# A fused attention and FP4 feed-forward layer on one core: fifty products into an unread bank, placed in TensorE's waits of the last two slots

## The chip, the core and the metric

The kernel runs on one core of a Trainium2 chip. The metric is the device time of one execution in microseconds (us). The kernel before takes 616.92 us, the median of three runs (615.69, 616.92 and 621.15 us). The profiled execution took 619.32 us. Engines: TensorE (PE, with its weight loads as PEld), VectorE (DVE), ScalarE (ACT), GpSimd (POOL) and the DMA queue that SyncE (SP) feeds.

## The reference, cut to what matters

Eight sequences of 512 rows by 256 columns go through two blocks, each with a residual connection:

```python
x = x + xattn(layernorm(x), ctx)      # causal self attention, cross attention, relu FFN, three layernorms
x = x + ffn(layernorm(x))             # SwiGLU, every operand quantised in blocks of 16 to FP4 and back
# ffn: gate = fp4(x) @ fp4(w_gate).T ; up = fp4(x) @ fp4(w_up).T
#      h = silu(gate) * up ; out = fp4(h) @ fp4(w_down).T
```

Widths: the model has 256 columns, the relu layer 1024, the FP4 layer 704. Every operand of the large products is split into a high and a low part (hi, lo), and three products (hi·hi, hi·lo, lo·hi) stand for one.

## The kernel before, in words

The rows are cut into 16 pairs of 256 rows (two blocks, t = 0 and t = 1, of 128 rows each). A pair goes through four stages, each one slot later than the one before: self-attention scores (lag 0), values and cross attention (lag A = 1), the relu feed-forward (lag F = 2), and the FP4 feed-forward (lag Q = 3), whose last part, the down projection, reaches into the slot after (lag Q + 1). So every slot works on up to five pairs at once. The work of each engine is written out by hand in the order in which it is to run (one `slot` function for each engine, called by `slots`, L281), and semaphores tie the engines together. An engine never passes a waiting instruction of its own: what stands behind it waits too.

The last slots are emptier. The pairs are numbered 0 to 15, PAIRS is 16, and the last slots are:

- slot 18 (PAIRS + 2): the second part of pair 14's down stage, and gate and up products of pair 15, nothing else;
- slot 19 (PAIRS + 3): the down stage of pair 15 alone.

TensorE's order in slot 18: `down(t=0)` of pair 14 (18 products of 256 columns, L1075 to L1077), `turn_hq(t=1)` (6 transposes, L886), `down(t=1)`, `turn_xq(t=0)` (2 transposes), `gate_up(0,0)` (12 products of 352 columns, L982 to L984), `turn_xq(t=1)`, `gate_up(0,1)`, `gate_up(1,0)`, `gate_up(1,1)`, then `turn_hq(t=0)` of pair 15. In slot 19: `down(t=0)`, `turn_hq(t=1)`, `down(t=1)`.

What these wait for: `turn_hq` waits for hq, which GpSimd writes (L457) at the end of a chain over four engines: silu on ScalarE, product, block maxima and reciprocals on VectorE, scaling on GpSimd (L451), absolute value on ScalarE (L673), rounding in two steps on VectorE (L1402, L1408). `down` waits until ScalarE has copied the turned rows out (hqT_hi, L694) and VectorE has formed the low part (hqT_lo, L1434). `turn_xq` waits for xq from GpSimd (L566); `gate_up(t, 0)` waits for xqT_hi (ScalarE, L658) and xqT_lo (VectorE, L1423). The result leaves with a VectorE addition (L1441) and a store (L387).

TR[1] is a PSUM bank of 512 columns, in which the attention stages turn their rows. After slot 17 nothing of the kernel reads or writes it.

Of the kernel before, what the change touches and what calls it, by code (L numbers as in the profile page):

```python
# [26 lines left out]
def layer_program(nc, x, ctx_in, w1, b1, w2, b2, g1, beta1, g2, beta2, g3, beta3,  # L27
                  w_gate, w_up, w_down, out):
    P = 128
# [8 lines left out]
    HALVES = S // ROWS  # L38
    PAIRS = B * HALVES
# [23 lines left out]
    with es:  # L63
        def sb(name, shape, dt=F32):
            return es.enter_context(nc.sbuf_tensor(name, shape, dt))
# [5 lines left out]
        w1_hi = sb("w1_hi", [P, KC, DFF], F32R)  # L71
# [102 lines left out]
        TR = [es.enter_context(nc.psum_tensor(f"TR{i}", [P, 512], F32)) for i in range(2)]  # L174
        O = [es.enter_context(nc.psum_tensor(f"O{i}", [P, 512], F32)) for i in range(2)]

        def bank(i):
            return R[:, 512 * i:512 * (i + 1)]
# [76 lines left out]
        def wait(eng, s, b, h, lag, k, j):  # L255
            mul, add = HALVES * k, k * (h - lag) + j
            if isinstance(b, int):
                if mul * b + add > 0:
                    eng.wait_ge(s, min(mul * b + add, k * PAIRS))
            else:  # L260
                assert FIRST * mul + add > 0
                eng.wait_ge(s, b * mul + add)
# [7 lines left out]
        def wait_batch(eng, s, b, k, j):  # L270
            if isinstance(b, int):
                if k * b + j > 0:
                    eng.wait_ge(s, min(k * b + j, k * B))
            else:
                assert FIRST * k + j > 0
                eng.wait_ge(s, b * k + j)

        def live(b, h, lag):
            return not isinstance(b, int) or 0 <= HALVES * b + h - lag < PAIRS
# [602 lines left out]
        def _(pe):  # L882
            mm = nc.tensor.matmul

            def turn(o, i):
                return nc.tensor.transpose(o, i, ident[:])  # L886
# [51 lines left out]
            def ready_for_scores(b, h):  # L938

                n = HALVES * b + h if isinstance(b, int) else None  # L940
                if n == 2:
                    pe.wait_ge(wq_lo, 2)
                if n == 3:
                    pe.wait_ge(wq_lo, 5)
# [13 lines left out]
            def turn_xq(b, h, t):  # L958
                wait(pe, xq_set, b, h, Q, T, t + 1)
                if h == 1 and t == 0:  # L960

                    wait_batch(pe, ctxT_set, b, 1, 1)
                for c in range(KC):
                    last = turn(TR[0][:, P * c:P * (c + 1)], xq[:, t, P * c:P * (c + 1)])
                last.then_inc(xq_turned, 1)

            def gate_up(b, h, t, s):
                if s == 0:
                    wait(pe, xqT_hi_set, b, h, Q, T, t + 1)
                    wait(pe, xqT_lo_set, b, h, Q, T, t + 1)  # L970
                if t == 0 and s == 0:
                    wait(pe, relu_set, b, h, F, FC, FC // 2)
                elif t == 0:
                    wait(pe, relu_set, b, h, F, FC, FC)
                else:
                    wait(pe, h_set, b, h, Q, 2 * T, s + 1)
                for m, done in ((0, gate_done), (1, up_done)):
                    o = bank(2 * s + m)[:, 0:GH]
                    cols = slice(GH * s, GH * (s + 1))
                    for c in range(KC):  # L980
                        xh, xl = xqT_hi[:, t, P * c:P * (c + 1)], xqT_lo[:, t, P * c:P * (c + 1)]
                        mm(o, xh, gu_hi[:, c, m, cols], start=(c == 0), stop=False)  # L982
                        mm(o, xh, gu_lo[:, c, m, cols], start=False, stop=False)  # L983
                        last = mm(o, xl, gu_hi[:, c, m, cols], start=False, stop=(c == KC - 1))  # L984
                    last.then_inc(done, 1)

            def turn_rows(b, h, lag, n, out_bank, done):
                for c in range(KC):
                    for t in range(T):
                        last = turn(out_bank[:, ROWS * c + P * t:ROWS * c + P * (t + 1)],  # L990
                                    n(t)[:, P * c:P * (c + 1)])
                last.then_inc(done, 1)
# [64 lines left out]
            def turn_hq(b, h, t):  # L1057
                wait(pe, hq_set, b, h, Q, T, t + 1)
                if t == 0:
                    wait(pe, h_set, b, h, Q, 2 * T, 2 * T)  # L1060
                else:
                    wait(pe, hqT_lo_set, b, h, Q, T, 1)
                for i in range(IC):
                    last = turn(R[:, TURNED + P * i:TURNED + P * (i + 1)], hq[:, t, P * i:P * (i + 1)])
                last.then_inc(hq_turned, 1)

            def down(b, h, t):
                wait(pe, hqT_hi_set, b, h, Q, T, t + 1)
                wait(pe, hqT_lo_set, b, h, Q, T, t + 1)

                wait(pe, z1_set, b, h, A - 1, T, t + 1)
                o = O[t][:, 0:D]
                for i in range(IC):
                    hi, lo = hqT_hi[:, t, P * i:P * (i + 1)], hqT_lo[:, t, P * i:P * (i + 1)]
                    mm(o, hi, wd_hi[:, i, :], start=(i == 0), stop=False)  # L1075
                    mm(o, hi, wd_lo[:, i, :], start=False, stop=False)  # L1076
                    last = mm(o, lo, wd_hi[:, i, :], start=False, stop=(i == IC - 1))  # L1077
                last.then_inc(down_done, 1)
# [47 lines left out]
            def turn_context(b):  # L1126
# [3 lines left out]
                                               ctx_rows[0:SC, P * c:P * (c + 1)], ident[0:SC, 0:SC])  # L1130
                last.then_inc(ctx_turned, 1)

            def turn_y0(b, h):
                wait(pe, ln_out[0], b, h, 0, T, T)
                turn_rows(b, h, 0, lambda t: y0[:, T * h + t, :], TR[1], y0_turned)
# [5 lines left out]
            def turn_z2(b, h):  # L1141
                wait(pe, ln_out[2], b, h, F, T, T)
                turn_rows(b, h, F, lambda t: z2[:, t, :], TR[1], n2_turned)
# [7 lines left out]
            def slot(b, h):  # L1151
                a, f, q = live(b, h, A), live(b, h, F), live(b, h, Q)
                q1, front = live(b, h, Q + 1), live(b, h, 0)
                if a:
                    values(b, h, 0)
                if f:
                    turn_z2(b, h)
                if a:
                    values(b, h, 1)
                if isinstance(b, int) and HALVES * b + h == Q:  # L1160
                    w_turn(4, FC, HEAD, 0)
                if q1:
                    down(b, h - 1, 0)
                if f:
                    ready_for_ff1(b, h)
                    ff1(b, h, (0,))
                if q1:
                    turn_hq(b, h - 1, 1)
                if f:
                    ff1(b, h, (1,))  # L1170
                if front:
                    turn_y0(b, h)
                if f:
                    ff1(b, h, (2, 3))
                if front:
                    ready_for_scores(b, h)
                    scores(b, h)
                    scores_rest(b, h)
                if q1:
                    down(b, h - 1, 1)  # L1180
                if f:
                    ff1(b, h, (4, 5))
                if q:
                    if isinstance(b, int) and HALVES * b + h == Q:
                        w_turn(5, FC + FC // 2, 0, 0)
                    turn_xq(b, h, 0)
                if f:
                    ff1(b, h, (6, 7))
                if q:
                    ready_for_gate_up(b, h)  # L1190
                    gate_up(b, h, 0, 0)
                    turn_xq(b, h, 1)
                    gate_up(b, h, 0, 1)
                    gate_up(b, h, 1, 0)
                if a:
                    turn_z1(b, h)
                if q:
                    gate_up(b, h, 1, 1)
                if a:
                    cross(b, h)  # L1200
                if f:
                    ready_for_ff2(b, h)
                    ff2(b, h, 0, range(FF2_CUT))
                if a:
                    turn_cross(b, h)
                if f:
                    ff2(b, h, 0, range(FF2_CUT, FC))
                if a:
                    cross_values(b, h)
                if f:  # L1210
                    ff2(b, h, 1, range(FF2_TURN))
                if q:
                    turn_hq(b, h, 0)
                if front and h == 0:
                    turn_context(b)
                if f:
                    ff2(b, h, 1, range(FF2_TURN, FC))
# [532 lines left out]
```

## Time and profile before

| | us |
|---|---|
| median of three runs | 616.92 |
| profiled execution, its own time | 619.32 |
| its span, first to last instruction | 617.3 |
| TensorE busy | 571.1 (93%) |
| VectorE busy | 497.1 (81%) |
| GpSimd busy | 390.8 (63%) |
| ScalarE busy | 378.0 (61%) |
| mean granted clock of TensorE, share of full speed | 0.972 |

The profile divides the span into 40 slices of 15.4 us. TensorE is at 9 tenths or more in nearly all of them, at 7 in the last but one and at 5 in the last. The granted clock is at full speed (2.4 GHz) except in a few of the first slices and in the last three, where it is partly at half (1.2 GHz). 79% of the chain that ended last is TensorE. In the timelines a product's row shows its start and its duration up to the end of its drain; neighbours overlap, so what a product costs in a train is the distance between starts.

### The profile page before, as it was taken

The numbers are of one execution on the slowest core, as the hardware profiler recorded it, in microseconds if no ns is written. First come the engines' busy times: TensorE is split into PE (matmuls) and PEld (weight loads), VectorE is DVE, ScalarE is ACT, GpSimd is POOL, SyncE is SP. The second block draws the span as 40 slices with busy tenths as digits, with TensorE's granted clock in tenths as the row PEclk, the third lists the DMA queues.
The fourth block names the chain that finished last, engine by engine and source line by source line (L and its number), as shares of the span: only waits on it lengthen the run. The fifth ranks groups of instructions, "written<-read, shape, count | busy, mean of one in ns | idle before, by whom it ended". The sixth has DMA issues, their size and how long they took to land.

```text
span 617.3 us, 12406 instructions
## 1 busy us (share of the span) xinstructions
PE 571.1 (93%) x4021; PEld 544.3 (88%) x4021; DVE 497.1 (81%) x1218; ACT 378.0 (61%) x781; POOL 390.8 (63%) x468
## 2 busy tenths in 40 slices
PE   4896779999999999999999999999999999999775
PEld 3785669999999999999999999999999999988665
DVE  5786869888888878888888888887888888787752
ACT  3565456675748676667658574867666765755331
POOL 3658556676666766686657667676667666665621
PEclk9998979999999999999999999999999999999886
DMA  7701001010100101010101010010101010000000
GB/s 230 226 2 35 1 1 43 1 53 1 44 19 2 53 1 61 0 51 0 59 0 51 0 33 27 0 51 0 59 2 35 2 35 3 17 2 18 10 9 17
DMA packets 18742, 19.30 MB, mean 31 GB/s; under 512 B 1536, under 2 KB 18192, under 8 KB 18704
## 3 DMA queue, kind: packets, MB, share of 16 engines
q1 hardware_dynamic: 18704, 18.82, 9.9%
q8 instruction: 20, 0.33, 0.2%
q14 instruction: 18, 0.15, 0.1%
HBM read 14.62 MB, written 4.19 MB: 30 GB/s over the span
## 4 chain that ended last, share of the span: by engine, by line
PE 79%; issue 6%; DVE 6%; POOL 5%; ACT 3%; DMA 0%; POOLq 0%; DVEq 0%; ACTq 0%
PE R L982 6%; PE R L984 6%; PE R L983 6%; PE TR L886 5%; PE O L1033 5%; PE O L1096 5%; PE R L1051 5%; PE R L1053 4%; PE R L1052 4%; PE O L1098 4%; PE O L1097 4%; PE R L886 4%; PE O L1075 3%; PE O L1077 3%; PE O L1076 3%
## 5 line engine op out<-in xcount | busy, mean ns | idle before, releaser
L445 POOL TENSOR_TENSOR rs<-mv,neg_half 128x1 f32<-128x1 f32 (+1 forms) x112 | 70.8, 642 | 32.9 <-DVE mv L1349 31.7
L982 PE MATMUL R<-gu_hi,xqT_hi 128*128 128x352 f32 x256 | 86.2, 337 | 2.4 <-ACT xqT_hi L658 1.0
L694 ACT ACTIVATE hqT_hi<-R 128x768 fp32r<-128x768 f32 x32 | 26.0, 813 | 98.1 <-PE R L886 98.1
L1051 PE MATMUL R<-y2T_hi,w_hi 128*128 128x256 f32 x256 | 78.3, 306 | 8.3 <-ACT e_full L723 4.2
L984 PE MATMUL R<-gu_hi,xqT_lo 128*128 128x352 f32 x256 | 83.1, 325 | 0.0
L983 PE MATMUL R<-gu_lo,xqT_hi 128*128 128x352 f32 x256 | 83.1, 324 | 0.0
L1096 PE MATMUL O<-w_hi,hT_hi 128*128 128x256 f32 x256 | 74.5, 291 | 2.4 <-POOL hT_lo L480 2.4
L1053 PE MATMUL R<-y2T_hi,w_lo 128*128 128x256 f32 x256 | 73.9, 289 | 0.0
L1052 PE MATMUL R<-y2T_lo,w_hi 128*128 128x256 f32 x256 | 73.8, 288 | 0.0
L451 POOL TENSOR_TENSOR hs<-hh,h_rec 128x704 f32<-128x704 f32 x32 | 44.5, 1392 | 45.9 <-DVE h_rec L1385 45.9
L1098 PE MATMUL O<-w_hi,hT_lo 128*128 128x256 f32 x256 | 71.9, 281 | 0.0
L1097 PE MATMUL O<-w_lo,hT_hi 128*128 128x256 f32 x256 | 71.8, 280 | 0.0
L1075 PE MATMUL O<-wd_hi,hqT_hi 128*128 128x256 f32 x192 | 61.4, 320 | 5.9 <-issue 5.9
L1051 PEld LDWEIGHTS R<-y2T_hi,w_hi 128*128 128x128 f32 x256 | 50.2, 196 | 9.5 <-ACT e_diag L717 5.7
L457 POOL TENSOR_TENSOR hq<-ha,h_div 128x704 f32<-128x704 f32 x32 | 44.6, 1393 | 20.2 <-DVE ha L1408 19.7
L1076 PE MATMUL O<-wd_lo,hqT_hi 128*128 128x256 f32 x192 | 55.9, 291 | 0.0
L1077 PE MATMUL O<-wd_hi,hqT_lo 128*128 128x256 f32 x192 | 55.9, 291 | 0.0
L683 ACT ACTIVATE hT<-R,b_fold 128x256 f32<-128x256 f32 x128 | 50.9, 473 | 3.4 <-PE R L1053 3.3
L982 PEld LDWEIGHTS R<-gu_hi,xqT_hi 128*128 128x128 f32 x256 | 48.7, 190 | 3.3 <-issue 2.0
L1096 PEld LDWEIGHTS O<-w_hi,hT_hi 128*128 128x128 f32 x256 | 48.4, 189 | 3.0 <-issue 2.6
L1052 PEld LDWEIGHTS R<-y2T_lo,w_hi 128*128 128x128 f32 x256 | 50.4, 197 | 0.0
L1053 PEld LDWEIGHTS R<-y2T_hi,w_lo 128*128 128x128 f32 x256 | 50.1, 196 | 0.0
(148 smaller groups left out, 1820.6 us busy)
## 6 DMA issues: line engine op xcount, KB each, us to landing
x_in<-in_x SPq DMA_DIRECT2D x16, 256.0 KB, 2.8
x_res<-in_x SPq DMA_DIRECT2D x16, 256.0 KB, 2.8
out<-x SPq DMA_DIRECT2D x32, 128.0 KB, 1.9
ctx_rows<-in_ctx SPq DMA_DIRECT2D x16, 64.0 KB, 2.5
hT<-in_L_xattn_w SPq DMA_DIRECT2D x1, 1024.0 KB, 7.2
hh<-in_L_xattn_w SPq DMA_DIRECT2D x1, 768.0 KB, 8.6
wd_raw<-in_L_ffn_w_down SPq DMA_DIRECT2D x1, 704.0 KB, 10.1
w_raw<-in_L_ffn_w_gate SPq DMA_DIRECT2D x1, 640.0 KB, 4.5
```

The source lines that it names most:

```text
L982: mm(o, xh, gu_hi[:, c, m, cols], start=(c == 0), stop=False)
L983: mm(o, xh, gu_lo[:, c, m, cols], start=False, stop=False)
L984: last = mm(o, xl, gu_hi[:, c, m, cols], start=False, stop=(c == KC - 1))
L1051: mm(o, w1_hi[:, c, cols], y2T_hi[:, c, :], start=(c == 0), stop=False)
L1052: mm(o, w1_hi[:, c, cols], y2T_lo[:, c, :], start=False, stop=False)
L1053: last = mm(o, w1_lo[:, c, cols], y2T_hi[:, c, :], start=False, stop=(c == KC - 1))
L1075: mm(o, hi, wd_hi[:, i, :], start=(i == 0), stop=False)
L1076: mm(o, hi, wd_lo[:, i, :], start=False, stop=False)
L1077: last = mm(o, lo, wd_hi[:, i, :], start=False, stop=(i == IC - 1))
L1096: mm(o, hi, w2_hi[:, f, :], start=False, stop=False)
L1097: mm(o, hi, w2_lo[:, f, :], start=False, stop=False)
L1098: last = mm(o, lo, w2_hi[:, f, :], start=False, stop=(f == FC - 1))
```

## The change

A function `keep_busy` is added. In the slot with the given number it issues `count` products of w1_hi's first 128 columns with w1_hi's first 512 columns (both of type fp32r, 128 x 128 by 128 x 512) into the bank TR[1]. They carry no semaphore and wait for none. It is called six times, at five places of the code: 42 products in slot 18 and 8 in slot 19, 50 together.

```diff
+            def keep_busy(b, h, slot_number, count):
+                if isinstance(b, int) and HALVES * b + h == slot_number:
+                    for _ in range(count):
+                        mm(TR[1][:], w1_hi[:, 0, 0:P], w1_hi[:, 0, 0:4 * P], start=True, stop=True)
...
                 if q1:
                     down(b, h - 1, 0)
+                    keep_busy(b, h, PAIRS + 2, 6)
...
                 if q1:
                     turn_hq(b, h - 1, 1)
+                    keep_busy(b, h, PAIRS + 2, 8)
+                    keep_busy(b, h, PAIRS + 3, 8)
...
                     turn_xq(b, h, 0)
+                    keep_busy(b, h, PAIRS + 2, 4)
...
                     gate_up(b, h, 1, 1)
+                    keep_busy(b, h, PAIRS + 2, 16)
...
                 if q:
                     turn_hq(b, h, 0)
+                    keep_busy(b, h, PAIRS + 2, 8)
```

TensorE at the start of slot 18, behind `down(t=0)` of pair 14 (the row above the first fill is its last product; what stands in brackets is what a row waits for):

```order
L1077 MATMUL O<-wd_hi,hqT_lo 128x256
L1137 MATMUL TR<-w_hi 128x512 x6
L886 MATMUL R<-ident,hq 128x128 [waits hqT_lo_set,hq_set]
L886 MATMUL R<-ident,hq 128x128 x5
L1137 MATMUL TR<-w_hi 128x512 x8
L1075 MATMUL O<-wd_hi,hqT_hi 128x256 [waits z1_set,hqT_lo_set,hqT_hi_set]
```

Before, the transposes (L886) stood right behind L1077, and L1075 right behind the transposes; now six and eight fills (L1137) stand between them.

TensorE around the end of slot 18 and the start of slot 19, before:

```order
L984 MATMUL R<-gu_hi,xqT_lo 128x352
L886 MATMUL R<-ident,hq 128x128 [waits h_set,hq_set]
L886 MATMUL R<-ident,hq 128x128 x5
L1075 MATMUL O<-wd_hi,hqT_hi 128x256 [waits z1_set,hqT_lo_set,hqT_hi_set]
L1076 MATMUL O<-wd_lo,hqT_hi 128x256
```

And with the change:

```order
L984 MATMUL R<-gu_hi,xqT_lo 128x352
L1137 MATMUL TR<-w_hi 128x512 x16
L886 MATMUL R<-ident,hq 128x128 [waits h_set,hq_set]
L886 MATMUL R<-ident,hq 128x128 x5
L1137 MATMUL TR<-w_hi 128x512 x8
L1075 MATMUL O<-wd_hi,hqT_hi 128x256 [waits z1_set,hqT_lo_set,hqT_hi_set]
L1076 MATMUL O<-wd_lo,hqT_hi 128x256
```

Each group of fills is ahead of the row whose wait it shares; no other row changed its place. On the other engines no instruction was added or moved.

## Rows read from the trace of the kernel before

**Rows 1.** Busy time of each engine in stretches, cut where the granted clock changes.

```profile
core 0: us, PE busy (x) PEld busy (x) DVE busy (x) ACT busy (x) POOL busy (x), PEclk, DMA share, GB/s
...
577.14:580.55 3.41, 0.88 (x6) 0.64 (x6) 2.17 (x9) 1.02 (x2) 2.37 (x4) 1.00 0.00 0
580.55:590.79 10.24, 8.61 (x35) 8.21 (x35) 5.71 (x15) 3.56 (x7) 4.32 (x7) 0.50 0.08 27
590.79:601.03 10.24, 6.14 (x40) 5.86 (x39) 7.16 (x13) 4.03 (x7) 2.78 (x2) 1.00 0.00 1
601.03:607.86 6.83, 4.89 (x23) 4.52 (x23) 2.92 (x4) 1.46 (x2) 2.78 (x2) 0.50 0.00 0
607.86:611.27 3.41, 1.47 (x13) 1.26 (x13) 1.29 (x2) 0.81 (x1) 0.00 (x0) 1.00 0.00 0
611.28:614.68 3.40, 3.32 (x17) 3.02 (x15) 0.05 (x1) 0.00 (x0) 0.00 (x0) 0.50 0.11 39
```

**Rows 2.** Timeline of PE, the high clock: start, duration, what ran, idle before.

```profile
start us, us, engine line op out<-in xcount [idle before <-releaser]
...
574.73 0.28 PE L1077 MATMUL O<-wd_hi,hqT_lo 128*128 128x256 f32 x1
...
576.48 0.27 PE L1077 MATMUL O<-wd_hi,hqT_lo 128*128 128x256 f32 x1
578.29 0.88 PE L886 MATMUL R<-ident,hq 128*128 128x128 f32 x6 [1.53 <-POOL hq L457]
...
591.00 0.32 PE L983 MATMUL R<-gu_lo,xqT_hi 128*128 128x352 f32 x1
...
596.43 0.32 PE L984 MATMUL R<-gu_hi,xqT_lo 128*128 128x352 f32 x1
```

**Rows 3.** Timeline of PE, waits and work of the last two slots.

```profile
581.20 0.55 PE L1075 MATMUL O<-wd_hi,hqT_hi 128*128 128x256 f32 x1 [2.03 <-issue]
...
585.17 0.63 PE L886 MATMUL TR<-ident,xq 128*128 128x128 f32 x2
586.78 0.63 PE L982 MATMUL R<-gu_hi,xqT_hi 128*128 128x352 f32 x1 [0.98 <-ACT xqT_hi L658]
587.21 0.50 PE L983 MATMUL R<-gu_lo,xqT_hi 128*128 128x352 f32 x1
...
590.14 0.50 PE L984 MATMUL R<-gu_hi,xqT_lo 128*128 128x352 f32 x1
590.44 0.56 PE L886 MATMUL TR<-ident,xq 128*128 128x128 f32 x2
...
600.85 1.42 PE L886 MATMUL R<-ident,hq 128*128 128x128 f32 x6 [4.09 <-POOL hq L457]
604.21 0.55 PE L1075 MATMUL O<-wd_hi,hqT_hi 128*128 128x256 f32 x1 [1.94 <-issue]
...
608.05 0.82 PE L886 MATMUL R<-ident,hq 128*128 128x128 f32 x6
610.81 0.36 PE L1075 MATMUL O<-wd_hi,hqT_hi 128*128 128x256 f32 x1 [1.94 <-issue]
...
614.18 0.41 PE L1077 MATMUL O<-wd_hi,hqT_lo 128*128 128x256 f32 x1
```

**Rows 4.** Timelines of DVE, ACT and POOL: what feeds those waits.

```profile
585.44 0.25 DVE L1397 RECIPROCAL x_rec<-x_div 128x16 f32<-128x16 f32 x1
...
586.26 0.42 DVE L1423 TENSOR_TENSOR xqT_lo<-TR,xqT_hi 128x256 fp32r<-128x256 f32 x1 [0.56 <-ACT xqT_hi L658]
...
587.88 0.62 POOL L566 TENSOR_TENSOR xq<-xa,x_div 128x256 f32<-128x256 f32 x1 [1.49 <-DVE xa L1418]
...
603.15 0.96 DVE L1434 TENSOR_TENSOR hqT_lo<-R,hqT_hi 128x768 fp32r<-128x768 f32 x1 [1.85 <-ACT hqT_hi L694]
...
605.91 1.39 POOL L457 TENSOR_TENSOR hq<-ha,h_div 128x704 f32<-128x704 f32 x1 [3.14 <-DVE ha L1408]
...
614.63 0.42 DVE L1441 TENSOR_TENSOR x<-O,w_raw 128x256 f32<-128x256 f32 x1 [3.60 <-PE O L1077]
```

## The prediction, made blind

> **What bounds the kernel now.** The page says that TensorE holds 79% of the chain that ended last, and the clock line drops in the last slices, so I read the end first. The windows, cut where the granted clock changes, show three falls from 2.4 to 1.2 GHz [rows 1]. The clock was high from 577.14 to 580.55 while TensorE did 0.88 us of work, six transposes, and was low for the next 10.24 us. It was high again to 601.03, of which TensorE worked 6.14 of 10.24 us with its longest wait (4.09 us) at the end, then low for 6.83 us. It was high to 607.86 + 3.41 = 611.27 with 1.47 us of work, then low to 614.68. In all 20.5 us of the last 37 ran at half clock, and TensorE worked in 16.8 of them (8.61 + 4.89 + 3.32).
>
> The waits ahead of and between these stretches are those of the two last slots: 1.53 us before the transposes at 578.29 [rows 2], 2.03 us before down(t=1) at 581.20, 0.98 us before gate_up at 586.78, 4.09 us before the transposes at 600.85, 1.94 us before down(t=0) at 604.21 and 1.94 us before down(t=1) at 610.81 [rows 3]. In each TensorE waits for other engines; the change fills exactly these six.
>
> **What a fill costs.** No row has 512 columns, so two widths are extrapolated. High clock, 256 columns: starts at 574.73 and 576.48, 15 steps, 0.1167 us each; 352 columns: 591.00 to 596.43, 34 steps, 0.160 us each [rows 2]. That is 0.00045 us a column, so 0.160 + 160 x 0.00045 = 0.231 us. Low clock, 352 columns: 587.21 to 590.14, 10 steps, 0.293 us [rows 3], 1.83 times the high one, so about 0.423 us. These two are the bounds: 0.16 below (no fill can be cheaper than the narrower product) and 0.423 above. I take 0.231, since the fills are there to run at high clock and the clock is high where the first of them stand (577.14 to 580.55 [rows 1]).
>
> **Fills against waits, at high clock.** 6 x 0.231 = 1.39 in 1.53; 8 x 0.231 = 1.85 in 2.03; 4 x 0.231 = 0.92 in 0.98; 16 x 0.231 = 3.70 in 4.09; twice 1.85 in 1.94. All fit, the last two with 0.1 us to spare, and the idle times count from the end of the drain, some 0.16 us after the train's last step, so a little more room is there. Cost 0. Their cover is the wait itself; where a wait shrinks, the fill is what comes late.
>
> **What the fills give.** If the clock stays high over the last 37 us:
>
> 1. *Slot 18 up to the second xq block.* down(t=1) starts at 581.20 as now, and takes 18 x 0.117 = 2.1 us instead of about 4. gate_up(0,0) does not gain all of it: xqT_lo on VectorE (L1423) stands behind x_rec, which ends at 585.69, so it would run at about 585.75 instead of 586.26 [rows 4], and gate_up(0,0) would start at about 586.25 instead of 586.78. Its 12 products end by 586.25 + 12 x 0.160 = 588.2. The next transposes need xq from GpSimd, 587.88 + 0.62 = 588.50 [rows 4], which hangs on x_rec and does not move. They start at 588.55 instead of 590.44 [rows 3]: **1.9 us** gained, on the path, since the gate and up products, silu, the quantising chain and hq all follow in the same distances (they ran at high clock from 590.79 on).
> 2. *Transposes of hq, t=0.* At low clock 3.36 us pass from their start to down (600.85 to 604.21); at high clock 2.76 (608.05 to 610.81) [rows 3]. **0.6 us**, sum 2.5: down(t=0) starts at 601.7.
> 3. *down(t=0) and the next transposes.* It takes 2.1 us and is done at 603.8. Now it ends about 608.05 and the transposes of t=1 follow at once, though hq has been there since 605.91 + 1.39 = 607.30 [rows 4]. Afterwards hq is what is late. Its chain runs through VectorE behind L1434, so it moves by 1.9 at least and by 2.5 at most; I take 2.3, as its first step also waits for GpSimd's scaling. hq is there at 605.0, the transposes start then, not at 608.05. Sum **3.0 us**.
> 4. *down(t=1).* From its start to VectorE's addition it takes 614.63 - 610.81 = 3.82 us now; at high clock 0.19 for the first step, 16 x 0.117, and 0.3 for the end make 2.37. **1.45 us.**
>
> Sum 4.5 us. The addition and the store behind it are unchanged. For the profiled execution: 619.32 - 4.5 = 614.8 us.
>
> That execution lies 2.4 us above the median. Where the clock falls is not fixed by the program alone, and an execution nearer the median may well have lost less of its end to the low clock. I bound the gain on the median by 1.9 (term 1 alone) and 5.0 (a run that lost a little more), and take 3.8: **613.1 us**, 0.6% faster.
>
> **A rule of the skill against it.** The clock fell at 580.55 although no wait before it was longer than 2.03 us [rows 3], and the 3.41 us ahead of it held 0.88 us of transposes [rows 1]. The Trainium skill, "TensorE: Matmul & The Clock Gate", section "Why this matters for your kernels", ties a drop to idle gaps of more than about 3 us between bursts of matmuls. By that rule only the 4.09 us wait could drop the clock, and the fills of the shorter waits would buy nothing. The trace disagrees: two of the three falls came after waits of 1.5 to 2 us with only transposes between.
>
> **Rivals.**
>
> - *The first fall has another cause and stays.* For it: its stretch has transposes, 26% busy, and waits that are each short. Against it: it is the emptiest stretch of the tail, and nearly all of its idle time is filled. Then term 1 is gone, and the four fills ahead of gate_up run at low clock: 4 x 0.423 = 1.69 against 0.98, 0.7 us late. Term 2 stands (0.6); hq moves by 0.4 only, so the transposes of t=1 come 1.1 earlier in all; term 4 gives 1.45. Sum 2.55 - 0.7 = 1.85: 615.1 us on the median. The rule named above would lead here. 8%.
> - *The fills outlast the waits (slower).* The mechanism: products into an unread bank do not hold the clock, or a 512-column product costs more than extrapolated; TensorE works in order, so real work stands behind the fills. It decides from 1.94 / 8 = 0.243 us a fill in the two tightest places and from 4.09 / 16 = 0.256 in the longest. At 0.423 us: 8 x 0.423 - 2.03 = 1.35; 1.69 - 0.98 = 0.7; 6.77 - 4.09 = 2.7; twice 3.38 - 1.94 = 1.45; together 7.6 us, and nothing gained: 624.5 us. For it: the margin between 0.231 and 0.243 is thin. Against it: a small excess costs only 8 x that excess at two places, under 0.5 us for 0.26 us a fill; the large cost needs the low clock, and the fills leave few idle stretches. 5%.
> - *The change does not do what it says*: the fills run in the waits, but what ends the waits is not nearer, or the clock is held and other engines set the pace. The rows say that steps 3 and 4 are TensorE's own time. Within 1 us of 616.9. 6%.
> - *Forecast*: 81%.
>
> **How the numbers follow.** About 1% (6.2 us) is what a measurement of this kernel can tell from no change. The forecast's own range is 616.9 - 5.0 to 616.9 - 1.9, 611.9 to 615.0, and three runs that spread over 5.5 us can move a median by 1 us either way: 610.9 to 616.0. Reaching to the first rival and most of the third gives 610.9 to 616.5, with the slower case left out. Faster by over 1% needs a gain of 6.2, beyond the sum of all terms, so it takes scatter as well: 0.08. Slower by over 1% is the second rival: 0.04. Within 1%: 0.88.
>
> **What the profile after would show.** Right: granted clock 1.00 in every window from 577 to the end, and no product of L1075 at 0.41 us; fills 0.23 us apart; the transposes of t=1 in slot 18 still at the same distance from their hq; gate_up's second pair of transposes waiting for GpSimd's xq, 1.9 us earlier; the last transposes waiting for hq after about 1 us idle; about 6 us between the start of down(t=0) and of down(t=1). Wrong: a low clock between down(t=1) and gate_up (first rival); fills at 0.42 us, or a product of L1075 or L886 that starts right behind a fill although its operands have been there (second); an end no nearer to hq of t=1 than now, at a high clock (third).

## The result, and the profile after

| | before | with the fills |
|---|---|---|
| median, 16 runs each | 619.59 us | 615.55 us |
| lowest to highest | 615.57 to 622.46 | 612.82 to 617.53 |
| profiled execution | 619.32 us | 612.82 us |
| ratio, 95% interval | | 0.9943, 0.9923 to 0.9963 |

The kernel is 0.57% faster, 4.0 us, and the interval excludes no change. With 13 further runs the median of the kernel before is 619.59 us; the three runs that the prediction had gave 616.92. So the gain came out about as forecast (3.8 us), and the time itself 2.4 us above the forecast: the base lies 2.7 us higher, the gain is 0.2 larger.

The page after: span, TensorE, and the granted clock in 40 slices (tenths of full speed).

```profile
span 610.9 us, 12506 instructions
...
PE 570.2 (93%) x4071; PEld 540.6 (88%) x4071; DVE 498.4 (82%) x1218; ACT 378.3 (62%) x781; POOL 391.0 (64%) x468
...
PE   4786859999999999999999999999999999999997
...
PEclk9789889999999999999999999999999999999999
```

50 instructions more, and the last slices of the clock line are at 9 (the digit for 90% or more). The windows of the tail, cut at the first fill and at the ends of slot 18's parts (columns as in [rows 1]):

```profile
core 0: us, PE busy (x) PEld busy (x) DVE busy (x) ACT busy (x) POOL busy (x), PEclk, DMA share, GB/s
574.66:584.00 9.34, 7.98 (x46) 5.99 (x44) 7.10 (x22) 3.70 (x6) 5.99 (x10) 1.00 0.05 16
584.00:592.63 8.63, 8.20 (x51) 7.94 (x51) 4.57 (x11) 2.66 (x6) 2.39 (x3) 1.00 0.05 16
592.63:600.00 7.37, 6.80 (x33) 5.17 (x33) 5.45 (x8) 3.82 (x5) 2.87 (x3) 1.00 0.00 0
600.00:608.10 8.10, 7.09 (x50) 6.05 (x48) 2.71 (x4) 0.81 (x1) 1.38 (x1) 1.00 0.05 18
```

No low clock anywhere, where [rows 1] had 20.5 us of it. TensorE's timeline after (a merged row's duration runs to the end of its last drain):

```profile
574.54 0.28 PE L1077 MATMUL O<-wd_hi,hqT_lo 128*128 128x256 f32 x1
574.66 1.57 PE L1137 MATMUL TR<-w_hi 128*128 128x512 f32 x6
576.37 0.87 PE L886 MATMUL R<-ident,hq 128*128 128x128 f32 x6
576.99 2.09 PE L1137 MATMUL TR<-w_hi 128*128 128x512 f32 x8
579.27 0.36 PE L1075 MATMUL O<-wd_hi,hqT_hi 128*128 128x256 f32 x1 [0.19 <-issue]
...
586.59 0.44 PE L886 MATMUL TR<-ident,xq 128*128 128x128 f32 x2 [0.28 <-POOL xq L566]
...
592.63 3.80 PE L1137 MATMUL TR<-w_hi 128*128 128x512 f32 x16
596.89 0.88 PE L886 MATMUL R<-ident,hq 128*128 128x128 f32 x6 [0.47 <-POOL hq L457]
...
599.71 0.36 PE L1075 MATMUL O<-wd_hi,hqT_hi 128*128 128x256 f32 x1
...
602.98 0.88 PE L886 MATMUL R<-ident,hq 128*128 128x128 f32 x6 [0.92 <-POOL hq L457]
...
605.79 0.36 PE L1075 MATMUL O<-wd_hi,hqT_hi 128*128 128x256 f32 x1
```

And VectorE's last addition:

```profile
608.17 0.42 DVE L1453 TENSOR_TENSOR x<-O,w_raw 128x256 f32<-128x256 f32 x1 [2.15 <-PE O L1077]
```

Measured from a common point, the start of the last product of pair 14's down(t=0) (576.48 before [rows 2], 574.54 after):

| event | before | after | gained | forecast |
|---|---|---|---|---|
| second xq block's transposes | 13.96 | 12.05 | 1.9 | 1.9 |
| down(t=0) of pair 15 | 27.73 | 25.17 | 2.6 | 2.5 |
| transposes of hq, t=1 | 31.57 | 28.44 | 3.1 | 3.0 |
| last addition | 38.15 | 33.63 | 4.5 | 4.5 |

Of the 6.5 us between the two profiled executions, 4.5 lie behind this point. The other 1.9 lie ahead of it, where the programs are the same.

### The profile page after: what moved, and what is told of

Its sections match the earlier page's. It is cut to its first block, busy times and chain, and to the rows that moved or that the text cites. A ratio compares the mean times of both kernels' runs of the same rounds, so it can differ in the third digit from the quotient of the medians.

```text
span 610.9 us, 12506 instructions
## 1 busy us (share of the span) xinstructions
PE 570.2 (93%) x4071; PEld 540.6 (88%) x4071; DVE 498.4 (82%) x1218; ACT 378.3 (62%) x781; POOL 391.0 (64%) x468
## 4 chain that ended last, share of the span: by engine, by line
PE 73%; DVE 7%; issue 6%; POOL 6%; ACT 2%; POOLq 0%; DVEq 0%; ACTq 0%
PE R L982 6%; PE R L984 5%; PE R L983 5%; PE O L1033 5%; PE TR L886 5%; PE O L1096 4%; PE O L1098 4%; PE O L1097 4%; PE R L1051 4%; PE R L1053 4%; PE R L1052 4%; PE R L886 3%; PE O L1075 3%; PE O L1077 3%; PE O L1076 3%
## 5 line engine op out<-in xcount | busy, mean ns | idle before, releaser
L451 POOL TENSOR_TENSOR hs<-hh,h_rec 128x704 f32<-128x704 f32 x32 | 44.5, 1392 | 44.6 <-DVE h_rec L1397 44.6
L1075 PE MATMUL O<-wd_hi,hqT_hi 128*128 128x256 f32 x192 | 58.9, 307 | 0.4 <-issue 0.2
L457 POOL TENSOR_TENSOR hq<-ha,h_div 128x704 f32<-128x704 f32 x32 | 44.5, 1392 | 19.9 <-DVE ha L1420 19.5
L1077 PE MATMUL O<-wd_hi,hqT_lo 128*128 128x256 f32 x192 | 53.7, 280 | 0.0
L1076 PE MATMUL O<-wd_lo,hqT_hi 128*128 128x256 f32 x192 | 53.7, 280 | 0.0
```

## The experiments

Five rounds each; "before" ran beside them on the same chip. The tail, the stretch that only the fills touch, is measured in each profile from slot 17's turn_hq(t=0) to the last addition: 614.63 - 571.66 = 42.97 us before, 608.17 - 569.71 = 38.46 us after.

**One group of fills, in the longest wait.**

```diff
-keep_busy(b, h, PAIRS + 2, 6)
-keep_busy(b, h, PAIRS + 2, 8)
-keep_busy(b, h, PAIRS + 3, 8)
-keep_busy(b, h, PAIRS + 2, 4)
 keep_busy(b, h, PAIRS + 2, 16)
-keep_busy(b, h, PAIRS + 2, 8)
```

(The kernel that ran keeps these lines with a count of 0, which issues nothing; so does the next one.)

> Only the 16 fills in the longest wait (4.1 us) are left; the 34 fills of the five short waits are gone. Theory (short waits also drop the clock): the clock falls at the start of slot 18 as before, so the 1.9 us of slot 18 are not gained; it is high through the transposes of hq, t=0 (0.6 us) and down(t=0) (0.5 us more), and down(t=1) gains between 0 and 1.45 us, depending on whether it falls again in slot 19. Together 1.1 to 2.5 us faster than before, and low-clock stretches remain in the profile after 577 us. Rival (the Trainium skill's rule on idle gaps over about 3 us): this one group of fills holds the clock, no fall in the tail, the full 4 us.

Measured: 617.69 against 618.38 us, ratio 0.9989 (0.9966 to 1.0013). Windows of its tail, cut where the clock changes:

```profile
577.00:581.42 4.42, 2.40 (x19) 1.96 (x18) 3.29 (x8) 0.43 (x1) 3.79 (x5) 1.00 0.00 0
581.42:588.24 6.82, 4.61 (x20) 4.23 (x20) 5.11 (x15) 3.31 (x7) 3.92 (x6) 0.50 0.07 22
588.25:608.72 20.47, 15.88 (x96) 14.26 (x96) 11.59 (x21) 7.24 (x12) 6.17 (x5) 1.00 0.02 7
608.73:613.90 5.17, 4.18 (x18) 3.92 (x18) 1.22 (x2) 0.00 (x0) 0.00 (x0) 0.50 0.07 25
```

The middle fall is gone, the first and the third are there, behind waits of at most 2.03 us with transposes between. That is against the rival, the Trainium skill's rule on idle gaps over about 3 us, by which this one group would have held the clock. The tail took 40.5 us, 2.5 less than before. The median moved by only 0.7 us, less than the 1.1 forecast, and its interval holds no change as well as 2.1 us: by the medians this group alone is not shown to gain.

**All groups but that one.**

```diff
-keep_busy(b, h, PAIRS + 2, 16)
```

> The five short waits are filled, the longest (4.1 us) is not. Theory: the first fall is gone (1.9 us gained), the fall in the long wait comes as before; eight fills behind the transposes then run at 0.42 us each, 3.4 us against a wait of 1.94, so 1.45 us late; the clock is back for down(t=1). Net gain 0.5 to 2.5 us. Rival by the rule on idle gaps over about 3 us: a wait of 4.1 us drops the clock at least once, but the short fills give nothing, so 0 gained or slower by up to 3 us.

Measured: 616.22 against 618.38 us, ratio 0.9959 (0.9936 to 0.9981). TensorE at the fall that is left:

```profile
599.12 1.54 PE L886 MATMUL R<-ident,hq 128*128 128x128 f32 x6 [4.10 <-POOL hq L457]
600.32 3.76 PE L1137 MATMUL TR<-w_hi 128*128 128x512 f32 x8
...
606.48 0.82 PE L886 MATMUL R<-ident,hq 128*128 128x128 f32 x6
607.05 2.08 PE L1137 MATMUL TR<-w_hi 128*128 128x512 f32 x8
```

Eight fills take 3.76 us at low clock and 2.08 at high. The slower rival's mechanism is therefore real, but it needs an unfilled fall ahead of it. The tail took 39.7 us, 3.3 less than before, so in this profile the short groups bring more than half of the gain by themselves; the median gained 2.2 us, within the 0.5 to 2.5 forecast.

**Transposes as fills**, two for each product.

```diff
-for _ in range(count):
-    mm(TR[1][:], w1_hi[:, 0, 0:P], w1_hi[:, 0, 0:4 * P], start=True, stop=True)
+for _ in range(2 * count):
+    turn(TR[1][:, 0:P], ident[:])
```

> Each fill is replaced by two transposes of the identity (128 columns each, about 0.11 us at high clock, so the same time in all). Theory (what counts is that TensorE is at work in the wait): same as the change, 4 us faster than before, clock 1.00 through the tail. Rival (the Trainium skill, TensorE: Matmul & The Clock Gate, Part 4: transposes do not count as TensorE activity in the same way): the clock falls as before, the transposes run at 0.21 us each, the long wait's 32 take 6.8 us, and the kernel is 3 to 8 us slower than before.

Measured: 616.34 against 618.38 us, ratio 0.9965 (0.9946 to 0.9984). Windows of its tail:

```profile
578.00:596.24 18.24, 16.23 (x116) 15.06 (x115) 11.95 (x31) 6.36 (x12) 8.63 (x12) 1.00 0.05 16
596.24:611.70 15.46, 13.54 (x114) 12.52 (x111) 8.16 (x11) 4.64 (x6) 4.26 (x4) 1.00 0.03 10
```

The clock stays high and the tail takes 38.5 us, as with products. Transposes hold this clock, so the rival is out. The median gained 2.0 us (interval 1.0 to 3.3), less than the 4 us forecast; the interval overlaps with the change's, so a difference between the two kinds of fills is not shown.

**Twice as many fills.**

```diff
-... 6 / 8 / 8 / 4 / 16 / 8
+... 12 / 16 / 16 / 8 / 32 / 16
```

> Every group of fills doubled (100 fills). Theory: a fill costs 0.225 us at high clock and real work stands behind it, so each group delays by what it exceeds its wait: about 1.5 us to the second block's gate products, 3.1 in the long wait, 1.4 ahead of down(t=0) and none at the transposes behind it as hq moves along, 1.4 ahead of down(t=1), less overlaps: about 6.5 us slower than the change, 2 to 3 us slower than before, with the clock at 1.00 throughout. Rival (fills have their own priority or are cheap, 0.13 us each): no more than 1 us slower than the change.

Measured: 621.33 against 618.38 us, ratio 1.0058 (1.003 to 1.0085). TensorE:

```profile
596.82 7.43 PE L1137 MATMUL TR<-w_hi 128*128 128x512 f32 x32
604.09 0.82 PE L886 MATMUL R<-ident,hq 128*128 128x128 f32 x6
604.66 3.92 PE L1137 MATMUL TR<-w_hi 128*128 128x512 f32 x16
```

The transposes start right behind the fills, with no wait: the fills are now what is late. The tail took 617.13 - 572.67 = 44.5 us, 6.0 more than the change (forecast 6.5), and the kernel is 3 us slower than before. Fills are work like any other on an engine that keeps its order.

**Narrow fills**, 32 columns.

```diff
-mm(TR[1][:], w1_hi[:, 0, 0:P], w1_hi[:, 0, 0:4 * P], start=True, stop=True)
+mm(TR[1][:, 0:32], w1_hi[:, 0, 0:P], w1_hi[:, 0, 0:32], start=True, stop=True)
```

> The same 50 fills at the same places, but 32 columns wide instead of 512, so each group takes a tenth of its wait or less. Theory (the time TensorE spends on columns holds the clock): the clock falls as before, nothing gained, within 0.7 us of before. Rival (an instruction in the wait is enough, or it is the presence of the fills that changes the order of things on the chip): as the change, 4 us faster.

Measured: 618.98 against 618.23 us, ratio 1.0014 (0.9993 to 1.0034). Windows, cut where the clock changes:

```profile
578.00:588.22 10.22, 6.27 (x51) 5.84 (x50) 7.99 (x22) 3.70 (x6) 6.86 (x10) 1.00 0.04 14
588.22:591.63 3.41, 3.41 (x13) 3.34 (x13) 0.85 (x2) 0.88 (x2) 0.71 (x2) 0.50 0.11 38
591.64:601.87 10.23, 7.82 (x56) 7.73 (x55) 7.12 (x13) 4.03 (x7) 2.77 (x2) 1.00 0.00 1
601.87:608.69 6.82, 6.40 (x30) 6.32 (x31) 3.01 (x4) 1.46 (x2) 2.77 (x2) 0.50 0.01 2
608.70:612.10 3.40, 2.26 (x21) 2.19 (x20) 1.29 (x2) 0.81 (x1) 0.00 (x0) 1.00 0.00 0
612.11:615.50 3.39, 3.39 (x17) 3.22 (x16) 0.00 (x0) 0.00 (x0) 0.00 (x0) 0.50 0.11 39
```

Three falls, and no gain in the median. The number of the fills, their order and their places are the change's, so it is not their presence that acts. The falls are not quite those of before: the first comes only at 588.22, behind the start of the gate products, 13.6 us of the tail are at low clock (20.5 before), and the tail took 42.1 us, 0.9 less than before.

One thing in the expectation is wrong: that each group takes a tenth of its wait or less. The longest group, and the transposes behind it:

```profile
597.53 1.85 PE L1137 MATMUL TR<-w_hi 128*128 128x32 f32 x16
601.79 1.50 PE L886 MATMUL R<-ident,hq 128*128 128x128 f32 x6 [2.41 <-POOL hq L457]
```

Sixteen narrow fills take 1.85 us, about 0.11 each, where the wide ones take 3.80. So the narrow groups still fill nearly half of their waits; the next kernel is one to set beside this.

**Half as many fills.**

```diff
-... 6 / 8 / 8 / 4 / 16 / 8
+... 3 / 4 / 4 / 2 / 8 / 4
```

> Every group of fills halved (25 fills), so each wait is about half filled. Theory: TensorE's share of work in the emptiest stretches lies between before and the change; some falls go and some stay, by where they happen to lie in an execution: 1.5 to 4 us faster than before. If the fills only had to break up the idle time (gap rule), the full 4 us and a profile with clock 1.00 throughout.

Measured: 615.85 against 618.23 us, ratio 0.996 (0.9934 to 0.9986). In its profile the clock is high through the tail, which takes 608.29 - 569.85 = 38.4 us. TensorE:

```profile
592.75 1.99 PE L1137 MATMUL TR<-w_hi 128*128 128x512 f32 x8
597.01 0.88 PE L886 MATMUL R<-ident,hq 128*128 128x128 f32 x6 [2.28 <-POOL hq L457]
...
603.10 0.88 PE L886 MATMUL R<-ident,hq 128*128 128x128 f32 x6 [0.93 <-POOL hq L457]
603.73 1.17 PE L1137 MATMUL TR<-w_hi 128*128 128x512 f32 x4
605.92 0.36 PE L1075 MATMUL O<-wd_hi,hqT_hi 128*128 128x256 f32 x1 [1.02 <-issue]
```

From the last slot's transposes to down(t=1) 2.82 us pass, with 1.02 us idle; in the change it was 2.81, with the wait filled. So the change's full groups cost nothing even in the tightest place, and half of them were enough in the profiled execution. Whether they are in every one the median (2.4 us gained, 3.2 for the change beside it) doesn't settle.

Beside the narrow fills this run says more. The four groups of slot 18 up to the longest wait take 4.7 us here (17 wide fills) and 4.2 us there (34 narrow ones), and what is left of the longest wait is 2.28 us here and 2.41 there. Yet here the clock stays high and there it falls three times, and the intervals of the two medians (615.85 and 618.98 us) do not meet. Such small differences in busy time and in idle time are an unlikely reason; the fills differ above all in their width. That a fill must be wide, and not only keep TensorE at work for as long, is argued from this pair and not tested by itself.

**The change again, and with groups in the program's first slots**, where [rows 1] does not reach: in the profile of before TensorE also waits 3.0 us at 50 us and 4.2 us at 87.

```diff
                 scores(1, 0)
+                keep_busy(1, 0, F, 6)
                 turn_z1(1, 0)
...
                 if f:
+                    keep_busy(b, h, HEAD, 16)
                     ff1(b, h, (4, 5))
```

> The change itself, on the same chip as the three kernels beside it: 4 us faster than before (0.9943, 0.992 to 0.996), and a tail without low clock.

> The change, and two more groups at the program's start: 16 fills in the 4.2 us wait at 82 to 87 us (ahead of ff1(4, 5) of slot 3) and 6 in the 3.0 us wait at 50 us. Theory: the falls behind these waits go (together 10 us at low clock in the profile before), of which TensorE's own time is up to a half: 1 to 3 us faster than the change, 5 to 7 faster than before. Rival (in the head other engines and loads set the pace): 0 to 0.5 us beyond the change.

Measured: the change 615.04 against 618.23 us, ratio 0.9949 (0.9923 to 0.9974); with the two groups 614.51 us, 0.9923 (0.9889 to 0.9957, 7 runs). The tails take 38.5 us each. The two intervals overlap. The six fills at 50 us did not do what was expected of them: the profile is at low clock from 52.7 and from 63.0 us, 3.4 us each. Three more kernels followed, each with the change in it: the group of slot 3 alone, a group of transposes at 18 us alone, and everything together, with 11 fills instead of 6 at 50 us and 8 more, into the other bank TR[0], in the 2.4 us wait at 62 us.

```diff
+            def keep_turning(count):
+                for _ in range(count):
+                    turn(TR[1][:, 0:P], ident[:])
...
                 values(0, 1, 1)
+                keep_turning(24)
                 turn_y0(0, 1)
```

> The change, and 24 transposes of the identity in the wait that ends at 18.4 us (2.0 to 4.5 us in the profiles so far), ahead of turn_y0(0, 1). Theory: the low clock that begins at 18.6 to 19.3 us in five of the ten profiles, for 7 to 17 us, is a fall of the same kind and goes; TensorE is short of time between 24 and 40 us, so 1 to 2 us faster than the change in the median, 5 to 6 faster than before, and less spread. Rival (the weight quantisation on VectorE and GpSimd sets the pace there): within 0.5 us of the change.

> The change, and 16 fills in the wait for e_full in slot 3 (4.2 to 4.9 us) alone. Theory: ff1(4, 5) to the first gate product takes 5.2 us as with both head groups, against 6.6 to 7.1 without; 1.5 to 1.8 us faster than the change, 5.5 faster than before. Rival (the 1.4 us are given back later in the head): within 0.5 us of the change.

> The change, both of the groups beside it, 11 fills in the 3.0 us wait at 50 us and 8 fills (into the other bank of that kind, TR[0]) in the 2.4 us wait at 62 us. Theory: no low clock after 20 us at all; sum of the parts, 3 to 4 us faster than the change, 7 to 8 faster than before (0.987 to 0.989). Rival: only the slot-3 group counts, 1.5 us beyond the change; or the 8 fills ahead of ff2 outlast their wait and cost up to 0.5 us.

| | us | before | ratio | interval |
|---|---|---|---|---|
| wait at 18 us | 615.93 | 618.66 | 0.9956 | 0.9929 to 0.9984 |
| wait in slot 3 | 612.64 | 618.66 | 0.9922 | 0.9895 to 0.9949 |
| all waits (6 runs) | 611.80 | 618.66 | 0.9906 | 0.987 to 0.9942 |

Slot 3, the change without its group (first row of ff1(4, 5) and first gate product):

```profile
87.50 0.55 PE L1051 MATMUL R<-y2T_hi,w_hi 128*128 128x256 f32 x1 [4.89 <-ACT e_full L723]
94.10 0.40 PE L982 MATMUL R<-gu_hi,xqT_hi 128*128 128x352 f32 x1 [1.23 <-ACT hT L683]
```

And with the group of slot 3:

```profile
85.54 0.36 PE L1051 MATMUL R<-y2T_hi,w_hi 128*128 128x256 f32 x1 [0.53 <-ACT e_full L723]
90.75 0.40 PE L982 MATMUL R<-gu_hi,xqT_hi 128*128 128x352 f32 x1 [1.23 <-ACT hT L683]
```

6.60 us there, 5.21 here: the fall behind the wait is gone, and 1.4 us with it. All three profiles with this group have 5.21 us, the ten without it 6.60 to 7.06. By the ratios (0.9949 and 0.9922) the kernel is about 1.7 us faster than the change; the two intervals still overlap a little, so it is the rows that show this gain. The group at 18 us brought nothing in the median, where 1 to 2 us were expected: its profile has 10.2 us of low clock begun at 24.4 us, behind the next wait (2.15 us), where six profiles without this group have 6.8 to 17.1 us of it begun at 18.6 to 19.9. All groups together leave 10.2 us of low clock in the head, from 22.6 and from 73.8 us, where none was expected after 20 us and the change's two profiles have 17 and 24. They are the fastest kernel measured here, 6.9 us faster than before by the medians and 5.8 by the ratio, less than the 7 to 8 expected; that they beat the slot-3 group alone, the intervals don't show.

## Why the prediction was right

- *The clock is what the waits cost.* Shown: the steps that gained are the ones whose rows went from low-clock to high-clock times; fills too narrow to hold the clock bring no gain; transposes, which do hold it, bring one.
- *Short waits count too.* Shown by the single group, whose first and third falls stayed. The first rival, a fall with another cause, is out: no fall of the tail is left in the two profiles of the change or in the four of kernels that contain it.
- *Fills against waits.* The price was 0.231 us. Measured: 16 of them take 3.80 us, less the last one's own 0.39 (the median of L1137's rows), over 15 steps 0.227. No group outlasted its wait: the transposes still wait 0.47 and 0.92 us for hq, and half the fills give the same distances.
- *Term 1.* 1.9 us. The second xq block waits 0.28 us for GpSimd, as forecast, so slot 18 gained what TensorE was late by and not the whole of what its products lost.
- *Terms 2 and 4.* 0.5 us (3.36 to 2.82) against 0.6, and 1.44 us (3.82 to 2.38) against 1.45.
- *Term 3.* After the change hq is what is late: 0.92 us of wait, about 1 forecast.
- *The slower rival.* It did not occur, but the doubled fills show its price (6.0 us beyond the change) and the fills behind an unfilled fall its mechanism.
- *From the profile to the median.* The median gained 4.0 us over 16 runs (interval 2.3 to 4.8) and 3.2 in the second comparison; that doesn't tell the forecast 3.8 from the profile's 4.5. The reason given for the smaller number, that the profiled execution was slow, fails: over 16 runs 619.32 is about the median. That 3.8 came so near is in part luck.
- *The base.* 613.1 was built on 616.92, a median of three runs that spread over 5.5 us. The prediction let scatter move such a median by 1 us either way; it was off by 2.7. The range held 615.55 because the gain came out near the forecast; with the smallest gain that the prediction allowed, 1.9 us, the same base would have given 617.7, outside it. So the mechanism and the gain were right, and that the time fell in the range is in part luck.

Open: why single executions differ by 5 us. The head's low clock differs from profile to profile (none from 16 to 42 us in the profile of before, 17.1 us with the transposes), but the mean granted clock, which is on record for each run, goes with the run's time only weakly: over the 35, 30 and 24 runs of the kernel before beside the experiments the correlation is -0.31, -0.21 and -0.39, at most about 15% of the variance. So most of the spread does not go with the mean clock, and its cause was not found. Nor was it settled why the single group gained 2.5 us in its profiled tail and 0.7 in the median.

## What to carry to other kernels

Where an engine's own work is slowed by its clock behind a wait, products into a bank that nobody reads can hold the clock; count them so that, at the high-clock price, they end before the wait does, and fill the short waits next to the long one too. Make them wide: 50 narrow ones, which took about as long as 25 wide ones, did not hold it. What comes back is only what that engine is late by: find the operand that is late next before pricing it. And take the base from more than three runs where they spread by more than the effect.

## What the runs showed of the hardware

The low clock came after waits of 1.5 and 2.0 us with six transposes between, at 580.55 before the change [rows 1] and at 581.42 with the single group. The Trainium skill, "TensorE: Matmul & The Clock Gate", section "Why this matters for your kernels", asks only that gaps stay under about 3 us, and these traces disagree. The Trainium skill, "TensorE: Matmul & The Clock Gate", Part 4, says that transposes do not count as TensorE activity in the same way; here 100 transposes in the six waits held 2.4 GHz through the tail as well as 50 products did. Only part of a wait had to be filled: half the groups left 2.28 us idle in the longest, at a granted clock of 1.00. But about the same time filled with products of 32 columns, 2.41 us left idle, did not hold it. A product of 32 columns took about 0.11 us in a train (1.85 us for 16), half of what one of 512 took (0.227).
